# Two FFN layers around causal attention on eight cores: moved row statistics, an earlier weight load, and PSUM evictions moved from VectorE to ScalarE during quantization

## What is computed

```python
x = x + 0.5 * ffn(layernorm(x), W1, b1, W2, b2)
x = x + attn(layernorm(x), w_q, w_k, w_v)
x = x + 0.5 * ffn(layernorm(x), W1, b1, W2, b2)

# ffn:  relu(x @ Q(W1).T + b1) @ Q(W2).T + b2, hidden width 4096
#       Q(W) = clip(round(W / (mean|W| + 1e-5)), -1, 1)
# attn: q, k, v = x @ w_q, x @ w_k, x @ w_v   (one head of width 1024)
#       softmax(causal(q @ k.T / 32)) @ v
```

## Time and profile before

| what | us |
| --- | --- |
| three executions | 3592.36, 3777.22, 3734.36 |
| their median | 3734.36 |
| the profiled execution | 3592.9 |
| its span on the slowest core (core 3) | 3590.9 |
| spans of the other cores | 3563.4 to 3580.1 |

### The profile page before, as it was taken

One profiled execution on the slowest core, in us unless ns is written; L12 is line 12 of the kernel. 1 busy time (PEld: TensorE's weight loads), 2 busy tenths in 40 slices (PEclk: granted clock), 3 DMA queues, 4 the chain that ended last, 5 costly groups with the idle time before them and its releaser, 6 DMA issues.

```text
span 3590.9 us, 41539 instructions; the slowest of 8 cores (3563.4 to 3590.9 us)
## 1 busy us (share of the span) xinstructions
PE 2701.7 (75%) x16308; PEld 1588.9 (44%) x16308; DVE 935.1 (26%) x1427; ACT 539.9 (15%) x959; POOL 12.0 (0%) x22
## 2 busy tenths in 40 slices
PE   0051498995966665998994998996876675799898
PEld 0020276474422232475483467475432222358467
DVE  2444422214312223222212222213402212321310
ACT  4121100102111112110101110102021112220110
POOL 0000000000000000000000000000000000000000
PEclk9975798997977887998997999998896877899899
DMA  5897510212010000212213131123010000121321
GB/s 176 255 289 227 201 71 33 86 71 48 1 24 1 0 1 24 94 71 82 83 71 117 59 129 48 65 80 68 1 24 0 0 0 24 47 74 45 118 94 71
DMA packets 72922, 267.10 MB, mean 74 GB/s; under 512 B 4898, under 2 KB 29731, under 8 KB 60452
## 3 DMA queue, kind: packets, MB, share of 16 engines
q1 hardware_dynamic: 64772, 235.08, 18.9%
q0 software_dynamic: 7968, 29.36, 3.4%
HBM read 243.45 MB, written 33.55 MB: 77 GB/s over the span
## 4 chain that ended last, share of the span: by engine, by line
PE 71%; DVE 11%; DMA 8%; ACT 5%; issue 4%; SPq 1%; DVEq 0%; ACTq 0%; POOLq 0%
PE pY L476 25%; PE pA L422 23%; PE pY L638 5%; PE pA L579 4%; PE pA L560 3%; PE pA L520 3%; PE pA L538 3%; DVE xm L352 2%; DVE ssum L317 2%; DMA stream<-w2t 2%; DMA stream<-w1t 2%; PE pT L360 2%; DVE amid L370 2%; PE pY L481 1%; ACT aw L603 1%
## 5 line engine op out<-in xcount | busy, mean ns | idle before, releaser
L422 PE MATMUL pA<-amid,aw 128*128 128x512 bf16 x4096 | 908.6, 386 | 214.8 <-DVE abig L436 144.6
L476 PE MATMUL pY<-aw,abig 128*128 128x256 bf16 x8192 | 945.9, 274 | 30.0 <-DVE stream L486 15.9
L476 PEld LDWEIGHTS pY<-aw,abig 128*128 128x128 bf16 x8192 | 784.4, 98 | 154.3 <-issue 34.4
L422 PEld LDWEIGHTS pA<-amid,aw 128*128 128x128 bf16 x4096 | 405.5, 99 | 715.6 <-issue 247.7
L436 DVE TENSOR_SCALAR abig<-pA,b1r_sb 128x512 bf16<-128x512 f32 x288 | 216.2, 751 | 672.5 <-PE pA L422 667.2
L486 DVE SCALAR_TENSOR_TENSOR stream<-pY,stream 128x256 f32<-128x256 f32 x256 | 108.6, 424 | 865.1 <-PE pY L481 864.8
L360 PE MATMUL pT<-id_sb,xm 128*128 128x128 bf16 x768 | 94.7, 301 | 299.8 <-DVE xm L352 299.8
L638 PE MATMUL pY<-abig,aw 128*128 128x512 bf16 x544 | 188.9, 506 | 97.1 <-ACT aw L630 97.1
L441 ACT ACTIVATE abig<-pA,b1r_sb 128x512 bf16<-128x512 f32 x224 | 154.3, 689 | 646.6 <-PE pA L422 642.9
L360 PEld LDWEIGHTS pT<-id_sb,xm 128*128 128x128 bf16 x768 | 72.3, 135 | 321.9 <-issue 321.8
L579 PE MATMUL pA<-abig,aw 128*128 128x512 bf16 (+3 forms) x640 | 157.6, 413 | 55.7 <-DVE stream L647 47.2
(11 more groups left out here) (58 smaller groups left out, 921.2 us busy)
## 6 DMA issues: line engine op xcount, KB each, us to landing
aw<-w1q SPq DMA_DIRECT2D x56, 1024.0 KB, 4.9
aw<-w2q SPq DMA_DIRECT2D x28, 2048.0 KB, 8.3
stream<-x SPq DMA_DIRECT2D x4, 4096.0 KB, 17.5
stream<-w1t SPq DMA_DIRECT2D x32, 512.0 KB, 9.1
stream<-w2t SPq DMA_DIRECT2D x32, 512.0 KB, 7.4
out<-stream SPq DMA_DIRECT2D x4, 4096.0 KB, 12.8
amid<-w1t SPq DMA_DIRECT2D x16, 512.0 KB, 8.2
aw<-w1t SPq DMA_DIRECT2D x16, 512.0 KB, 8.4
```

The lines of the kernel that those rows point to most:

```text
L422: w.op("tensor", lambda e, stat=stat, bk=bk, ci=ci, hf=hf: e.matmul(bk[:], stat, xlng[:, 0, ci, hf * 512:(hf + 1) * 512], start=(ci == 0), ...
L476: w.op("tensor", lambda e, stat=stat, bank=bank, buf=buf, fc=fc: e.matmul(bank[:, 0:256], stat, buf[:, fc, :], start=(fc == 0), stop=False ...
```

## The change

- `ln_stats` for attention is no longer one call for 16 tiles. Each group of the first feed-forward phase calls it for its 8 tiles at the end of its own down projection, so before `ln_tr` of the next group or of attention.
- `ln_stats` for group 0 of the second feed-forward phase is moved from the start of that phase into attention, behind row tile 7.
- In the first group of all, `fs` 0 to 3 are evicted by DVE alone, as before, and `fs` 4 to 7 by ACT alone.
- The loads of wk and wv have separate counts, and only V waits for wv. The load of wq is issued behind K and ahead of V.

```diff
-                if g == 0 and pre_marks is None:
-                    if is_p1:
-                        xw = load_x_group(s, 0)
-                        ln_stats(tiles, [xw], [xw, ("sV", 1)])
-                    else:
-                        ln_stats(tiles, None, [gates["p2v"][0]])
+                if g == 0 and pre_marks is None and is_p1:
+                    xw = load_x_group(s, 0)
+                    ln_stats(tiles, [xw], [xw, ("sV", 1)])
...
-                        allv = (fs_hook is not None and g == 0)
-                        eng = "vector" if (par == 0 or allv) else "scalar"
-                        sem = "sV" if (par == 0 or allv) else "sS"
+                        if fs_hook is not None and g == 0:
+                            use_v = fs < FS // 2
+                        else:
+                            use_v = (par == 0)
+                        eng = "vector" if use_v else "scalar"
+                        sem = "sV" if use_v else "sS"
...
                 gates["w1"] = [w.g("sT"), w.g("sT")]
 
+                if is_p1:
+                    ln_stats(tiles, [("sV", c["sV"])], [("sV", c["sV"])])
...
-            ln_stats(list(range(NT)), None, [w.g("sV")])
             p2marks = ln_tr(list(range(NT)), p2_dest)
 
-            for wi, wt in ((0, wk_t), (1, wv_t)):
-                w.dma("gpsimd", wkb[:, wi], wt.ap().rearrange("(c p) d -> p c d", p=128),
-                      "dG", wait=[gates["aw"][0]])
+            w.dma("gpsimd", wkb[:, 0], wk_t.ap().rearrange("(c p) d -> p c d", p=128),
+                  "dG", wait=[gates["aw"][0]])
             kv_dg = w.g("dG")
+            w.dma("gpsimd", wkb[:, 1], wv_t.ap().rearrange("(c p) d -> p c d", p=128),
+                  "dG", wait=[gates["aw"][0]])
+            wv_dg = w.g("dG")
...
+            w.dma("gpsimd", wkb[:, 0], wq_t.ap().rearrange("(c p) d -> p c d", p=128),
+                  "dG", wait=[w.g("sT")])
+            wq_dg = w.g("dG")
+
             for tb in range(NT):
...
-                            wait=[gates["pa"][bi], mk[0], mk[1]] if ci == 0 else None,
+                            wait=[gates["pa"][bi], wv_dg, mk[0], mk[1]]
+                            if ci == 0 else None,
...
-            w.dma("gpsimd", wkb[:, 0], wq_t.ap().rearrange("(c p) d -> p c d", p=128),
-                  "dG", wait=[w.g("sT")])
-            wq_dg = w.g("dG")
...
+                if qt == TPG - 1:
+                    gv = w.g("sV")
+                    ln_stats(list(range(TPG)), [gv], [gv])
```

## The result

The changed kernel is faster by 1.2%: the ratio of its time to that of the kernel before is 0.9883, with a 95% interval from 0.9869 to 0.9898. That is less than 2%, but clear of the noise. In us, some 42 of 3594. Its profiled execution took 3547.93 us against 3592.9, with a span of 3545.9 us against 3590.9. The forecast was 3534 us, 59 us less. Both kernels have some executions in which one die runs at a lower clock and takes some per cent longer; all ratios here leave them out.

The account below looks back on a forecast made before the run. The kernel was taken as bound by matmuls, with holes where PE waits. Terms of -28.5, -33.8, +3.0 and +0.4 us summed to -58.9 us from 3592.9, giving 3534 us, 1.6% less; range 3505 to 3568.

Parts of the forecast that it names:

- Part 1: First group: ACT evicts fs 4 to 7 while DVE quantizes W2, leaving x as what is late next; -28.5 us.
- my upper bound of 24.0: Load of x for group 1: at worst in a row with one W2 load, 15.9 + 8.1 us, landing at 430.6.
- its own signs: First group: eviction change called wrong if quantization ends after 410 or x lands after 431.
- the lower end of its range: First group's eviction change: smallest gain given as 17 us, of a range from 17 to 35.5.
- Part 2: Start of attention's Q block: wq loaded beside V, so the waits for it go; -33.8 us for both sequences.
- the cover of 56 us: V's 256 matmuls, beside which wq is loaded, were to last 56 us, four times the load.
- Part 3: Attention statistics: two calls of 11.65 us replace one of 21.8, the one at the turn not hidden; +3.0 us.
- Part 4: Last phase's group 0 statistics moved behind row tile 7: 12.94 us removed, a Q block stop added; +0.4 us for both sequences.
- the upper bound of +4: Moving the last phase's group 0 statistics into attention: bounds of -2 and +4 us for each sequence.
- Clock gives back: Attention entered without the stop keeps TensorE at full speed; 12.8 us per sequence, 3508 us; chance 0.20; sign 0.05 clock change.
- Part 1 brings little: Quantization loses 14 us to two W1 loads and x lands at 430.6 or beyond; 3562 us; chance 0.13.
- Slower: PE stops in row tile 8's Q block and its clock stays low until attention ends; 3664 us at 0.6; chance 0.05.

Follow-up runs that it names:

- alone -33.6: Kernel before with only the wq load moved ahead of the loop over V; ratio 0.9882, 33.6 us less by the stages.
- alone +4.8: Kernel before with only the attention statistics split into one 8-tile call behind each group's down projection; 3590.49 us in one execution, 4.8 us lost by the stages.
- alone +8.6: Kernel before with only the last phase's group 0 statistics moved behind row tile 7; 3604.89 us in one execution, 8.6 us lost by the stages.
- kernel with spread statistics: Parts 1 and 2, plus statistics issued one tile at a time behind down-projection evictions or attention maxima; ratio 0.9632, median 3456.25 us.
- parts 1, 2 or 3 alone: Kernel before with one edit each: ACT evicting fs 4 to 7, ratio 0.9941; early wq load, 0.9882; attention statistics by groups, 3590.49 us.
- the W1 loads left out: Parts 1 and 2, without the first group's W1 loads for fs 6 and 7, so part of the result is wrong; quantization took 115.5 us.
- W2 held back: Parts 1 and 2, with the first group's first two W2 loads waiting for x; x in flight 15.0 us, turn 273.8 us behind the summation's end.

## Why the prediction was right, and which terms were off

**Direction, mechanism and size of the whole.** Faster, within 2%, inside the range; 42 us instead of 59. All four parts gave less than forecast (by 7.5, 0.3, 1.4 and 7.8 us), so no error made up for another.

**Part 1, forecast -28.5, measured -21.0.** The path was as forecast: quantization, x, statistics, eviction, PE. Two terms were too small. The quantization grew by 5.9 us, not 3: I had taken a value near the lower end because the engines were free for a third of the time. But DVE waits for each chunk, so the time of each load counts, not the engines' average. And x took 23.2 us in the median (27.7 on core 3), not 20.0, and passed my upper bound of 24.0 on four of the eight cores. The bound counted one W2 load; the trace has two before x has landed, as the second follows on the same counter at once, 15 to 18 us behind x on every core. That is a likely reason for the bound's being too low, not a shown one: it does not tell why x took 20.2 us on one core and 28.9 on another. The two terms make up 6.1 of the 7.5 us missing. By its own signs this part was wrong: on core 3 x landed at 443.3, past 431, and quantization ended at 412.24, past 410 (of its 8.7 us, 5.6 are the late end of the summation, see below). And the lower end of its range was added up wrongly: x in a row with W2 (27.5) and 14 us of quantization leave 13.5, not 17.

**Part 2, forecast -33.8, measured -33.5** (alone -33.6 by the stages). The waits and the clock behind them were read from rows, and the cover of 56 us was ample.

**Part 3, forecast +3.0, measured +4.4** (alone +4.8). Right in kind: moved, not hidden. At the turn 11.5 and 11.7 us against 11.65; at the start of attention 9.5 and 9.3 us came back, not 10.2.

**Part 4, forecast +0.4, measured +8.2** (alone +8.6), each sequence some +4.1, just past the upper bound of +4. The step that was too small is what follows the stop, priced at two table loads alone. The stop itself was near: 8.50 us of waiting, and a block 11.2 us longer against the 10.6 forecast. The two table loads came, with 1.28 us each. But the row tile behind the stop lost 3.0 us, not 1.3: beyond the table load, its second burst of products with V took 3.4 to 3.6 us over the cores, where it had taken 1.89 on all of them, with a granted clock of 0.63 against 0.86 in the stretch around it (1172.25 to 1186.20, and 1186.50 to 1198.69 before).

The next phase lost 3.1, not 1.3. Beyond the table load, 1.45 us lie in its first up projection, whose matmuls run from 1398.67 for 113.57 us in the changed kernel and from 1421.18 for 112.12 in the kernel before, at a granted clock of 0.97 against 0.99. That loss need not come from the stop, 250 us earlier. In the kernel with spread statistics, which has no stop at row tile 8, the same up projection is 0.9 us longer than before in the median (114.7 against 113.8 us to the first down matmul, 115.3 in the changed kernel and 115.2 with part 4 alone). With parts 1, 2 or 3 alone, with the W1 loads left out and with W2 held back, all of which keep the statistics between attention and that `ln_tr`, it takes 113.8 us as before. So most of the loss goes with taking the statistics away from there; why was not separated.

**Table loads.** By the Trainium skill (ScalarE: Activation LUTs, section What ACT_TABLE_LOAD costs) each switch would bring a drain that doubles it. In the Q block ACT's load starts at 1151.04 and DVE's first eviction at 1152.85, which leaves 1.8 us for the load, the square root and L343. There is no room for the drain between them, so it added nothing to the path here.

**The rivals.** *Clock gives back*: no. Over attention as a whole the granted clock of core 3 went from 0.82 and 0.78 in the two sequences to 0.81 and 0.82, less than the 0.05 that was named as the sign. From the first Q block's scores to row tile 8 the first sequence took 115.0 us in the median against 117.0, the second 121.7 against 117.7, and cores of one kernel differ by 7 us there. *Part 1 brings little*: in part, 7.5 us of its 28.5. *Slower*: no; behind row tile 9 attention takes 164.5 us as before (165.1, 164.9). On core 3 the second sequence gained 11.3 us there, because cores 2 and 3 had been slow in the kernel before (175.8 and 175.9 against 164.8 to 165.0 on the others). That is no effect of the change, and most of the 17 us between the two sequences, by which the prediction widened its range, were of this kind.

**What was no effect.** The summation of W2 ended 4.2 us later in the changed kernel. None of the kernels of this study has an edit that acts before it, and in their profiles it ended between 278.9 and 286.8 us in the median, 283 in the middle. So the kernel before had a quick start in its profiled execution, by some 3 us, and the 4.2 us are no term of the change.

## What to carry to other kernels

Work that stands alone between two bursts of matmuls gains nothing by being moved to another such place; it has to be cut up and laid under matmuls: moved, the row sums of parts 3 and 4 cost some 12 us; spread, with those of the loaded x and of the last group, they gave some 78. When a wait is taken away, price the next transfer with all that will then be in flight beside it, the followers in its queue included. An issue that waits holds up whatever stands behind it on its queue, as SP's did with W1.

## What the runs showed of the hardware that I had not expected

Two transfers for one consumer went faster one behind the other than side by side: x in 15.0 us (median) and then W2 in 8.5 (429.62 to 438.11, core 3), where side by side x took 23.2 to 26.7 in the median. Two 1 MB loads stretched a chain of loads by 5 to 6 us with the DMA engines free for a third of that stage. And a stop of 8.5 us cost PE 2.3 us in the 32 matmuls behind it (9.59 against 7.29), and another 1.6 us in the second burst of products of the next row tile (3.51 against 1.89).
